# A third PSUM bank for the first matmuls of the MLP's units, and xa's transposes moved to the bank of the attention product

## What is computed

```python
# x: 8 sequences of 512 tokens (ids); D = 128 channels
h = relu(causal 2-tap depthwise conv of fake-quantised embeddings)       # _L0_tok_ref
h = h + ssm(layernorm(h))             # a linear recurrence with 4 x 64 states, then C and D
# the last part, per token:
xf = layernorm(h)
normed = (xf - mean(xf)) / sqrt(var(xf) + 1e-5) * ln_g + ln_b
x_attn = normed @ attn_w.T + attn_b + xf                  # the "attention product" and xa
tok = x_attn split into 2 x 8 groups of 256 tokens, group e goes to expert e
g = gelu(tok @ fc1_w[e].T + fc1_b[e])                     # 128 -> 512
y = g @ fc2_w[e].T + fc2_b[e]                             # 512 -> 128
out = h + gelu(y @ next_w.T + next_b)
```

## Time and profile before

| what | us |
|---|---|
| median of 3 runs (lowest, highest) | 182.64 (182.56, 182.87) |
| the profiled execution | 182.76 |
| its span in the trace | 180.9 |
| TensorE busy | 163.6 (90% of the span) |
| VectorE busy | 131.6 (73%) |
| ScalarE busy | 95.1 (53%) |
| GpSimd busy | 92.8 (51%) |

### The profile page before, as it was taken

How to read it: one execution, slowest core, us unless ns; L and a number is a source line. 1 busy time by engine, 2 the same in 40 slices (tenths; PEclk the granted TensorE clock), 3 DMA queues, 4 the chain that set the end, 5 groups by cost and what they waited for, 6 DMA issues and landing times.

```text
span 180.9 us, 3374 instructions
## 1 busy us (share of the span) xinstructions
PE 163.6 (90%) x1123; PEld 134.0 (74%) x1123; DVE 131.6 (73%) x405; ACT 95.1 (53%) x220; POOL 92.8 (51%) x152
## 2 busy tenths in 40 slices
PE   0587999999999899997999989999999999998993
PEld 0175785678664359765666889999999999996992
DVE  0869994484532077679987598997989898648983
ACT  3026993444123313020333775977869686796691
POOL 3107666299940000040040487696978969698700
PEclk9999999999999999999999999999999999999999
DMA  4994000000000000000000000000010100101013
GB/s 137 416 424 177 2 4 0 2 2 4 0 0 0 0 4 0 0 0 2 4 0 0 0 0 4 0 34 30 0 58 2 62 0 4 58 2 60 25 37 116
DMA packets 2325, 7.53 MB, mean 42 GB/s; under 512 B 254, under 2 KB 892, under 8 KB 2052
## 3 DMA queue, kind: packets, MB, share of 16 engines
q1 hardware_dynamic: 2162, 7.18, 10.1%
q10 hardware_dynamic: 146, 0.13, 0.3%
HBM read 5.22 MB, written 2.10 MB: 40 GB/s over the span
## 4 chain that ended last, share of the span: by engine, by line
PE 61%; DVE 11%; ACT 10%; POOL 8%; issue 6%; DMA 2%; ACTq 0%; POOLq 0%; DVEq 0%
PE bank L1161 9%; PE bank L1107 7%; PE bank L1181 7%; PE bank L975 6%; PE bank L1028 5%; PE bank L1034 5%; PE bank L1104 4%; PE bank L1127 3%; PE bank L928 3%; POOL hid_p L464 3%; ACT gel L573 2%; DVE u L698 2%; ACT hid_p L597 2%; PE bank L951 2%; PE bank L999 2%
## 5 line engine op out<-in xcount | busy, mean ns | idle before, releaser
L464 POOL TENSOR_TENSOR hid_p<-hid_f,hid_p 128x256 fp32r<-128x256 f32 x52 | 37.3, 743 | 17.0 <-ACT hid_p L597 15.4
L595 ACT ACTIVATE hid_f<-bank,pa 128x256 f32<-128x256 f32 x64 | 30.8, 486 | 18.5 <-PE bank L1161 17.7
L1161 PE MATMUL bank<-xaT_p,fc_p 128*128 128x256 f32 x192 | 36.1, 298 | 1.2 <-ACT hid_f L595 0.2
L447 POOL TENSOR_TENSOR rstd<-spread,neg_half 128x8 f32<-128x8 f32 x8 | 13.2, 1645 | 39.4 <-DVE spread L833 39.4
L1181 PE MATMUL bank<-hid_p,out_hi 128*128 128x256 f32 x128 | 32.3, 287 | 1.1 <-POOL hid_p L464 0.8
L1161 PEld LDWEIGHTS bank<-xaT_p,fc_p 128*128 128x128 f32 x192 | 26.7, 189 | 2.9 <-ACT hid_p L597 1.6
L1181 PEld LDWEIGHTS bank<-hid_p,out_hi 128*128 128x128 f32 x128 | 23.2, 188 | 2.0 <-POOL hid_p L464 1.9
L597 ACT ACTIVATE hid_p<-bank,pa 128x256 fp32r<-128x256 f32 x48 | 23.4, 488 | 0.0
L1107 PE MATMUL bank<-pb,xh 128*128 128x128 f32 x128 | 19.5, 275 | 0.0
L513 ACT ACTIVATE X<-bank 128x512 f32<-128x512 f32 x12 | 7.2, 597 | 21.4 <-PE bank L1034 21.4
L1181 PE MATMUL bank<-hid_p,out_lo 128*128 128x256 f32 x64 | 17.9, 279 | 0.0
(11 more groups left out here) (127 smaller groups left out, 337.4 us busy)
## 6 DMA issues: line engine op xcount, KB each, us to landing
fc_w<-in_fc SPq DMA_DIRECT2D x2, 2048.0 KB, 12.2
out<-res SPq DMA_DIRECT2D x7, 256.0 KB, 2.0
pa<-in_pack_a SPq DMA_DIRECT2D x1, 407.0 KB, 3.5
pb<-in_pack_b SPq DMA_DIRECT2D x1, 320.0 KB, 4.2
out<-res SPq DMA_DIRECT2D x2, 128.0 KB, 1.7
pc<-in_pack_c ACTq DMA_DIRECT2D x1, 128.5 KB, 3.1
pw<-in_pack_a SPq DMA_DIRECT2D x1, 64.0 KB, 3.8
emb_w<-in_emb SPq DMA_DIRECT2D x1, 62.5 KB
```

What stands on the lines that cost most here:

```text
L464: nc.gpsimd.tensor_tensor(hid_p[1][:, half, c, :], hid_f[:, m % HID_SLOTS, :], hid_p[0][:, half, c, :].bitcast(F32), ALU.subtract).then_in ...
L595: full = nc.scalar.activation(hid_f[:, m % HID_SLOTS, :], src, ACT.Gelu, bias=bias)
L1161: last = mm(bank[5 + n % 2][:, 0:HALF], fc1_p[w][:, e * HID + c * P:e * HID + (c + 1) * P], xaT_p[m][:, b % 2, half, :], start=(k == 0), s ...
```

## The change

Three things. `fc1_part` cycles over banks 5, 6 and 3 by the unit's number over the whole run, and waits for the unit three before its own instead of two; ScalarE reads from the same bank. In round 7 the parity test that picks the kind of wait follows the number of the unit waited for. xa's transposes go into bank 4, where the attention product has just been read, and ScalarE (L611) and VectorE (L814) read them there; `transpose_xa` drops its waits for `fused_lo_ready` and `xaT_lo_ready`. `transpose_h`, which writes bank 4 next, waits for `xaT_lo_ready` of the batch before in place of `xa_ready`.

```diff
--- before.py
+++ after.py
@@ -337,6 +337,9 @@
         def fuse_bank(e):
             return bank[(0, 1, 4, 5, 2, 3, 4, 3)[e]]
 
+        def fc1_bank(m):
+            return bank[(5, 6, 3)[m % 3]]
+
         def out_bank(b, half):
 
 
@@ -590,7 +593,7 @@
                                 act.wait_ge(o_done, 2 * (j - 1) + half + 1)
                             e = expert(j, half)
                             bias = pa[:, PA["fc1_b"]][:, e * HC + c:e * HC + c + 1]
-                            src = bank[5 + n % 2][:, 0:HALF]
+                            src = fc1_bank(m)[:, 0:HALF]
 
                             full = nc.scalar.activation(hid_f[:, m % HID_SLOTS, :], src, ACT.Gelu, bias=bias)
                             if j < DVE_ROUND:
@@ -610,7 +613,7 @@
                                 act.wait_ge(fc1_done, 8 * (b - 1))
                             nc.scalar.activation(
                                 xaT_p[0][:, b % 2, :, :].rearrange("p s (i k) -> p s i k", i=T),
-                                bank[3][:].rearrange("p (i s k) -> p s i k", i=T, s=2),
+                                bank[4][:].rearrange("p (i s k) -> p s i k", i=T, s=2),
                                 ACT.Identity, bias=attn_c[:]).then_inc(xaT_ready, 1)
                         b = j + 2
                         if n == 3 and 0 <= b < NB:
@@ -813,7 +816,7 @@
                             view = "p (i k) -> p i k"
                             last = nc.vector.scalar_tensor_tensor(
                                 out=xaT_p[1][:, b % 2, half, :].rearrange(view, i=T),
-                                in0=bank[3][:].rearrange("p (i s k) -> p s i k", i=T, s=2)[:, half],
+                                in0=bank[4][:].rearrange("p (i s k) -> p s i k", i=T, s=2)[:, half],
                                 scalar=attn_c[:],
                                 in1=xaT_p[0][:, b % 2, half, :].bitcast(F32).rearrange(view, i=T),
                                 op0=ALU.add, op1=ALU.subtract)
@@ -1114,7 +1117,7 @@
                     if b == 0:
                         pe.wait_ge(fused_lo_ready, 7)
                     else:
-                        pe.wait_ge(xa_ready, b)
+                        pe.wait_ge(xaT_lo_ready, b)
                     for q in range(NQ):
                         s = slice(q * CH, (q + 1) * CH)
                         last = nc.tensor.transpose(bank[4][:, s], h[:, b, s], ident)
@@ -1129,13 +1132,9 @@
 
                 def transpose_xa(b):
                     pe.wait_ge(xa_ready, b + 1)
-                    if b == 0:
-                        pe.wait_ge(fused_lo_ready, NE)
-                    else:
-                        pe.wait_ge(xaT_lo_ready, b)
                     for q in range(NQ):
                         s = slice(q * CH, (q + 1) * CH)
-                        last = nc.tensor.transpose(bank[3][:, s], xa[:, s], ident)
+                        last = nc.tensor.transpose(bank[4][:, s], xa[:, s], ident)
                     last.then_inc(xa_t_done, 1)
 
                 def fc1_part(b, n):
@@ -1148,8 +1147,8 @@
                             pe.wait_ge(x_ready[1], NP * (RUN - 1))
                             pe.wait_ge(last_ready[1], RUNS)
                             pe.wait_ge(fused_lo_ready, NE)
-                    before = 8 * b + n - 2
-                    if before >= LAST and n % 2 == 0:
+                    before = 8 * b + n - 3
+                    if before >= LAST and (before - LAST) % 2 == 0:
                         wait_high(pe, before)
                     elif before >= 8 * DVE_ROUND:
                         pe.wait_ge(full_ready, before + 1 - 8 * DVE_ROUND)
@@ -1158,7 +1157,7 @@
                     for k, (w, m) in enumerate(PARTS):
                         if n == 0 and m == 1:
                             pe.wait_ge(xaT_lo_ready, b + 1)
-                        last = mm(bank[5 + n % 2][:, 0:HALF], fc1_p[w][:, e * HID + c * P:e * HID + (c + 1) * P],
+                        last = mm(fc1_bank(8 * b + n)[:, 0:HALF], fc1_p[w][:, e * HID + c * P:e * HID + (c + 1) * P],
                                   xaT_p[m][:, b % 2, half, :], start=(k == 0), stop=(k == len(PARTS) - 1))
                     last.then_inc(fc1_done, 1)
 
```

## The result

The changed kernel takes 181.84 us (median of 6, 181.76 to 182.35), the kernel before 182.66 us (182.24 to 182.87). The ratio is 0.9965, 95% interval 0.995 to 0.998: 0.64 us faster by the ratio, between 0.37 and 0.91. The forecast was 182.1 within 181.5 to 182.8. The profiled run of after took 181.82 us with a span of 180.0, against 182.76 and 180.9.

What follows compares the result with a forecast made beforehand. TensorE was taken as the bound, busy 10.67 of a middle round's 10.78 us. 2 x 0.14 + 2 x 0.12 = 0.52 us off the 182.64 us median gave 182.1 us, range 181.5 to 182.8.

Steps and rivals of the forecast that it cites:

- The bank wait at unit 5: Rounds 1 to 5: `fc1_part` of unit 5 stops waiting for unit 3's second Gelu, 0.38 us each (round 5: 0.45).
- `hT` (0.21 left): TensorE's `attn` loads next wait for ScalarE's `hT` copy, leaving 0.21 of the 0.38 us.
- GpSimd's low half (0.14): Third matmul of `out_part` of unit 3 waits for GpSimd's low half: the tightest limit, leaving 0.14 us.
- `xh` (0.24): `mixer_out` of the next round waits for `xh`, allowing 0.24 us.
- Sum 0.52: Total gain in the loop: 0.14 us each in rounds 1 and 2, 0.12 each in rounds 3 and 4.
- Round 5 gives nothing: Unit 43's load already waits for GpSimd's low half, so the 0.45 us at unit 5 becomes a longer wait there.
- The tail gives 0: Rounds 6 and 7: TensorE arrives sooner but waits longer for GpSimd and VectorE; 0, within 0.2 us either way.
- Bank 4 costs nothing: xa's transposes in bank 4: `transpose_h`'s new wait for `xaT_lo_ready` is met 1.0 us ahead, so 0.
- Rival D: Loop through GpSimd is already as long as the round; the wait moves from ScalarE to GpSimd: 182.6 us, chance 0.24.
- Rival B: GpSimd's low half isn't tight; `attn` limits, 0.21 in four rounds, tail's 0.2 may come: 181.6 to 181.8, chance 0.12.
- Rival E: Tail: one more VectorE CAST falls under a GpSimd step on the shared port, up to 1.1 us: 183.2, chance 0.10.

Runs made afterwards that it cites:

- e2: The changed kernel with bank 3 serving only unit 5 of each round, all other units on two banks: 182.04 us, ratio 0.9963.
- e3: The changed kernel with GpSimd's power in `rstd` replaced by a multiplication (output not the function's, only times read): 180.42 us, ratio 0.9878.
- e5: The changed kernel with unit 3's low half directly behind `rstd` on GpSimd in rounds 0 to 4: 181.62 us, ratio 0.9939.
- e6: The changed kernel with unit 3's low half first on GpSimd and ScalarE's `hT` copy ahead of unit 3's Gelus: 181.38 us, ratio 0.9931.
- e7: The changed kernel with GpSimd's `res` of batch 5 moved behind unit 54's low half in round 6: 181.31 us, ratio 0.9923.
- e10: The kernel before (two banks) with only `res` of batch 5 moved behind unit 54's low half: 182.26 us, ratio 0.9984.
- e1: The changed kernel with the third bank taken back and xa's transposes kept in bank 4: 182.73 us, ratio 1.0003.
- e4: The kernel before with GpSimd's power in `rstd` replaced by a multiplication (output not the function's, only times read): 181.55 us, ratio 0.9943.
- e8: The changed kernel with GpSimd's `res` of batch 5 moved behind unit 50's low half in round 6: 182.03 us, ratio 0.9958.

## Why the prediction was right, point by point

- *The bank wait at unit 5 is what the third bank removes, in five rounds.* Right: L1160 waits for no Gelu after, and e2 gives the whole gain with the bank at that unit alone.
- *Behind it come `hT` (0.21 left), GpSimd's low half (0.14) and `xh` (0.24).* Right for GpSimd, which comes first: rounds of 10.66 us with it and of 10.56 without it (e3 and e5) are 0.13 and 0.23 under 10.79. `hT` and `xh` follow, at 0.21 and 0.24 by my reading, and the floor without GpSimd is 10.55 to 10.56 with `hT`'s wait and without it (e5, e6). So `xh`'s size is borne out; that `hT` comes ahead of it is not, since the two lie within the hundredths of a reading.
- *Sum 0.52, from 0.14, 0.14, 0.12 and 0.12.* The marks give 0.49 in these rounds, each within 0.03 of its term.
- *Round 5 gives nothing.* Right: 9.54 and 9.55 us, and unit 43's load waits, [0.24 <-POOL hid_p L467] at 160.62. But I named only this wait. The mark at the end of round 5 stands behind a second one, for VectorE's `xa`, in both kernels (before, then after):

```profile
161.84 1.36 DVE L789 TENSOR_SCALAR xa<-bank,rstd,shift 128x128 f32<-128x128 f32 x4
...
163.25 0.42 PEld L1138 LDWEIGHTS bank<-pc,xa 128*128 128x128 f32 x4
```

```profile
159.53 0.20 POOL L459 TENSOR_TENSOR ratio<-ratio,rstd 128x4 f32<-128x4 f32 x1
...
159.82 1.13 DVE L784 SCALAR_TENSOR_TENSOR bank<-h,ratio,bank 128x128 f32<-128x128 f32 x4 [2.37 <-PE bank L1130]
...
160.99 1.37 DVE L792 TENSOR_SCALAR xa<-bank,rstd,shift 128x128 f32<-128x128 f32 x4
```

  The loads start at 161.84 + 1.36 + 0.05 = 163.25 and at 160.99 + 1.37 + 0.05 = 162.41. `xa` follows L784, which starts as GpSimd's second `ratio` step ends (159.73), so both waits hang on GpSimd's `rstd`; with the cheap one round 5 takes 9.07 us (e3).
- *The tail gives 0, within 0.2 either way.* Right: it gave 0.09, which is there already at unit 54's low half: that starts 7.67 us after the last mark, before 7.75, behind a low half of unit 52 that takes 0.75 us instead of 0.84. The reason given, that unit 54's low half waits for `res` and the cast under it, is what e7 shows by moving `res`. I had not seen that 0.57 us lay ready for the third bank behind it (e7 and e10).
- *Bank 4 costs nothing.* Right: e1. No load of L1123 waits for L817. In this kernel the rule of the Trainium skill's page "PSUM — Partial Sum Buffer" (section "PSUM bank collisions raise a hardware error") that one bank be guarded as a whole costs nothing, since the guard is ready 1.0 us ahead.
- *Rival D, only the wait's name changes:* it holds for round 5 and not for the others, whose fall from 10.79 to 10.66 us excludes it. e4 alone would not, since with two waits equally tight a shorter row of GpSimd would give nothing either. *Rival B* needed GpSimd's end to be softer than its row; the load at 128.65 sits on it to 0.01 us. *Rival E* did not come in the changed kernel, but its mechanism is real: e8 has a subtraction of 1.41 us under `res`, and a tail 0.71 us longer than e7's.
- The median fell by 0.82 us, the loop by 0.56. The rest is not explained by the change. The two profiled runs differ by 0.36 at 11 us already, and the interval of the ratio, 0.37 to 0.91 us, takes in 0.56.

## What to carry to other kernels

Here a removed wait was worth the least room among what comes behind it in the loop, and not its own length: 0.38 us of waiting were worth 0.13. List the next waits with their rooms before the change, by the starts of weight loads against the ends of their releasers; the list also says what to mend next, and here moving unit 3's low half and `res`, with `hT` first beside them, took the ratio from 0.9965 to 0.9902. Where the gain of one edit is small, look for the engine that swallows it, as the same bank was worth 0.57 us in the tail instead of 0.09 once `res` had left the way of unit 54's low half.

## What the runs showed of the hardware

A VectorE cast of 256 columns takes 0.28 us alone, and up to 1.39 us when it starts during a GpSimd step with SBUF operands (the `res` of 1.48 us, before). A subtraction goes from 0.43 us to 0.86 under a step of 0.75 us (after, 167.83 under 167.67), and to 1.41 us under one of 1.34 (e8). In each of these the VectorE step ends 0.1 to 0.3 us behind the GpSimd step. The Trainium skill, page "SBUF — State Buffer", section "Who interferes with whom", says that of a VectorE step in a two-port mode, which a cast can be in, and a GpSimd step the first to issue has the shared ports for the whole instruction; of a `tensor_tensor` with both inputs in SBUF it says that it contends with GpSimd's reads. These numbers agree. e7 against e8 shows that the order of the same steps is worth 0.7 us in the tail.
